# Moving due times in a hand-planned cross-attention and feed-forward kernel: when x1 is written, when the last batch is stored, and where each gathered head is loaded and split

## The chip, the cores and the metric

The kernel runs on one core of one Trainium2 chip. The metric is the device time of one execution in microseconds (us); lower is better. Engines: PE is TensorE, DVE VectorE, ACT ScalarE, POOL GpSimd, SP SyncE (here it only issues DMAs).

## The reference

Eight batches, each with x and ctx of 512 channels by 2048 columns, all float32. Per batch:

```
xn  = layernorm(x, over the 2048 columns)
t   = Wt @ ctx ;  p = Wp @ xn ;  g = Wg @ ctx            (xattn with q = xn, k = v = ctx)
att = sum over each group of 64 channels of p * g        (one number per group)
y   = Wz (per group) @ (att * t)
x1  = x + (y - mean)/sqrt(var) * gn_w + gn_b + ctx       (mean, var per group)
u   = layernorm(x1)[:, perm]          -> 16 heads of 128 columns
out = x1 + (gelu(u_h @ up_h) @ down_h)[:, unperm]        (up_h 128x512, down_h 512x128)
```

## The kernel before, in words

Every matrix product is made in float32 accuracy with three passes: both operands are split into a rounded high part (`_hi`, a copy on ACT) and the rest (`_lo`, a subtraction on DVE), and PE multiplies low by high, high by low and high by high. All products have 512 columns.

A batch i has two stages. In the attention stage PE builds S = x ctx^T over 16 slices of columns (`s_mm`), then y in four quarters (`y_mm`), then p·g through S (`v_mm`). Meanwhile Z holds y; after the group statistics (`g_mean`, `g_var_a`, `g_root` on POOL, `g_var_b`) DVE writes x1 into Z in eight pieces of 128x1024 (`x1_piece`, L1134), ACT squares them (`square_x1`, L959), and `sum_sq`, `root_x1`, `shift_x1`, `xln2` (L966) normalise. `turn` (L1159) transposes Z, four tiles for each of four quarters, and `store_x` writes the transposed batch to DRAM in four DMAs a quarter; from there single heads are gathered by the permutation. The stores of batches 0 to 6 are issued by POOL (L1246), those of batch 7 by SP (L1317).

The feed-forward stage follows each attention stage on PE. It works through groups g; a group is one head of one earlier batch: 16 groups in batches 2 to 6, 8 in batch 1, none in batch 0, and 40 in batch 7, which also has to finish its own heads. Weights of a head are used for two groups (two batches) while two batches are at hand, and for one group in most of batch 7. One group is, by engine:

- POOL: `gather` (indirect DMA of 256 KB from DRAM into a slot of FB, L1240), `resid` (a multiplication and an addition of 128x512, L1252 and L1255), `scatter` (indirect DMA to the output, L1260). A slot of FB is gathered anew six groups later, once its scatter has landed.
- ACT: `g_hi` (cast into GG, L973), and for each of two halves p `gelu` (two activations of 128x1024, L980 and L981).
- DVE: `g_lo` (L1164), two `h_lo` (L1169), `add_r` (L1175).
- PE: for each half six matmuls `up_mm` (L888) and six `dn_mm` (L903).
- SP: `load_w` (L1338) loads half the weights of a head (512 KB) as soon as the head two before has used that half; `load_x` (L1305) and `load_s` load the next batch's x, and its columns for S.

The order is not found at run time. The function `plan()` gives every task a due time in units (a unit is the time of 12 matmuls), sorts all tasks by it, and each engine's program is that list filtered to its own tasks, in order. Semaphores alone decide when a task starts; the due time only decides what it stands behind on its engine. Engines work strictly in order, so a task that waits holds all behind it. `base[i]` is the start of batch i, f0 = base[i] + 36 that of its feed-forward stage (464 for batch 7). Group g has its `up_mm` halves due at f0+2g-1 and f0+2g, its `dn_mm` halves at f0+2g+1.5 and f0+2g+2.5; `gelu` is due 0.6 and `h_lo` 1.2 units behind `up_mm`, `g_lo` at f0+2g-2.1.

`X1_UNIT[1 if i == 1 else 2 if last else 0]` says in the groups of which numbers the eight `x1_piece` stand: (2,3,5,6,8,10,11,13) for batches 2 to 6, (2,2,3,4,4,5,6,6) for batch 1 and (2..9) for batch 7. The piece is due at f0+3.25+2·number, which is right behind the second `h_lo` of group number+1.

Of the kernel before, what the change touches and what calls it, by code (L numbers as in the profile page):

```python
# [26 lines left out]
TURN = [(15.9, 19.0, 22.3, 25.5)] + [(10.2, 15.0, 19.6, 24.2)] * 6  # L27
# [2 lines left out]
S_EARLY = ([(-1 + 0.2 * dt, 0.5 + 0.2 * dt) for dt in range(4)],  # L30
           [(2.0, 2.5), (2.25, 2.75), (3.0, 3.25), (3.5, 3.75)])
S_LOAD = (-13, -10, -7, -2.8, -1, 3.2, 4.8, 6.8)
X1_UNIT = ((2, 3, 5, 6, 8, 10, 11, 13), (2, 2, 3, 4, 4, 5, 6, 6), (2, 3, 4, 5, 6, 7, 8, 9))
S_FIRST = ((-5.9, -4.9, -3.9, -2.9), (-9.9, -7.9, -5.9, -3.9))
S_LATE = {4: 2.55, 5: 2.8, 6: 3.3, 7: 4.4}

# [1 line left out]
def units(i):  # L38

    if i == 0:  # L40
        return []
    if i == 1:
        return [(h, [0]) for h in range(8, 16)]
    half = [8 * (i % 2) + h for h in range(8)]
    if i == 2:
        half = half[6:] + half[:6]
    ws = [(h, [i - 2, i - 1]) for h in half]
    if i == B - 1:
        rest = [8 * ((i + 1) % 2) + h for h in range(8)]
        ws += [(h, [i - 1]) for h in rest[:6]] + [(h, [i - 1, i]) for h in rest[6:]]  # L50
        ws += [(h, [i]) for h in range(ND) if h not in rest[6:]]
    return ws
# [20 lines left out]
def plan():  # L73
# [10 lines left out]
    def put(t, stage, *a):  # L84
        tasks.append((t, len(tasks), stage, a))
# [462 lines left out]
    for k in range(8):  # L548
        t = 15 + 2.6 * k
# [4 lines left out]
    for h in range(4):  # L554
        t = 38 + 4 * h
# [5 lines left out]
    base = [0, 36, 88] + [88 + 68 * k for k in range(1, B - 2)]  # L561
    f = 0
# [3 lines left out]
    for i in range(B):  # L566
        s0 = base[i]
        y0, v0, f0 = s0 + 16, s0 + 32, s0 + 36
        first = i == 0
        for k, h in enumerate((4, 5, 6, 7) if i == 2 else ()):  # L570
            put(y0 + (2.5, 5.2)[k // 2], load_raw, h)
            put(y0 + 5.6 + 1.8 * k, w_hi, h)
            put(y0 + 5.7 + 1.8 * k, w_lo, h)
            put(y0 + 5.8 + 1.8 * k, keep_w, h)
        for j in range(8):
            put(s0 + (S_LOAD[j] if i > 1 else 0.3 if (i, j) == (1, 2) else 2 * j - (5 if i or j else 10)), load_s, i, j)
        for dt in range(ND):
            t = s0 + (dt - 2.6 if i < 2 else S_FIRST[i > 2][dt] if dt < 4 else S_LATE.get(dt, dt - 2.6))
            put(t, s_hi, i, dt)
            put(t + 0.2, s_lo, i, dt)  # L580
            for c1 in range(NT):
                put(s0 + (dt + 0.25 * c1 if i < 2 or dt > 3 else S_EARLY[c1 // 2][dt][c1 % 2]), s_mm, i, dt, c1)
        for q in range(NQ):
            for ct in range(NT):
                t = s0 + 2.2 + 3.3 * ct + 0.8 * q if i == 2 else s0 + (4 * q + ct) * 0.85 + 0.9
                t = 10.4 + 1.4 * ct + 0.22 * q if first else s0 + 9.3 + 1.6 * ct + 0.4 * q if i == 1 else t
                put(t, bn_x, i, ct, q)
        if first:
            for ct in range(NT):
                put(5.4 + 1.7 * ct, load_x, i, ct)  # L590
        put(y0 + 2, aggr_x, i)
        put(y0 + 2.1, root_x, i)
        late = 1.0 if i == 1 else 0
        for q, t in enumerate((s0 + 9, s0 + 11, s0 + 13, y0 + 1.5 + late)):
            put(t, load_c, i, q)
        put(y0 + (9 if i == 2 else 2.5 + late), load_wg, i)
        for q, t in enumerate((y0 - 3, y0 + 0.4, y0 + 4.3, y0 + 8.3)):
            put(t, y_hi, i, q)
            put(t + 0.2, y_lo, i, q)
        for q, t in enumerate((y0 - 1, y0 + 1.2, y0 + 2.6, y0 + 4.6)):  # L600
            for ct in range(NT):
                put(t + 0.25 * ct + late, add_c, i, q, ct)
        put(y0 + 5.8 + late, sum_c, i)
        put(y0 + 5.9 + late, store_sum, i)
        put(y0 + 7.6 + late, spread_sum, i)
        for c1 in range(NT):
            put(y0 + 11.3 + 0.6 * c1, s_fix, i, c1)
            put(y0 + 11.5 + 0.6 * c1, s_evh, i, c1)
            put(y0 + 12.2 + 0.6 * c1, s_evl, i, c1)
        for q in range(NQ):  # L610
            for ot in range(NT):
                put(y0 + 4 * q + ot, y_mm, i, q, ot)
            for pr in range(2):
                t = y0 + 4 * q + 2 * pr + 2
                put(t, y_ev, i, q, pr)
                for e in range(2):
                    put(t + 0.6 + 0.5 * e, bn_y, i, q, 2 * pr + e)
        if i:
            put(y0 + 1, load_wph, i)
            put(y0 + 12.1, load_wpl, i)  # L620
        for ot in range(NT):
            put(v0 + ot + (0.5 if i and ot == NT - 1 else 0), v_mm, i, ot)
            put(v0 + ot + (1.4 if i and ot == NT - 1 else 0.95), v_att, i, ot)
        put(v0 + 3.4, aggr_y, i)
        put(f0 + 1.2, g_mean_mm, i)
        put(f0 + 1.25, g_mean, i)
        put(f0 + 2.3, g_var_mm, i)
        put(f0 + 2.35, g_var_a, i)
        put(f0 + 2.4, g_root, i)
        put(f0 + (3.9 if first else 5.25), g_var_b, i)  # L630


        last = i == B - 1
        for k in range(8):
            ct, hf = k // 2, k % 2
            t = f0 + 5 + 0.8 * k if first else f0 + 3.25 + 2 * X1_UNIT[1 if i == 1 else 2 if last else 0][k] + 0.01 * k
            put(t, x1_piece, i, ct, hf)
            put(t + (0.9 if first else 1.2) if first or last else base[i + 1] + 0.9 + 0.55 * k, square_x1, i, ct, hf)
            if hf and not last:
                put(base[2] - 1.5 + 3.3 * ct if i == 1 else t + 0.1, load_x, i + 1, ct)  # L640
        put(f0 + (4.1 if first else 5.26), mean_x1, i)
        e = f0 + 12 if first else f0 + 22.8 if last else base[i + 1] + 5.4
        put(e, sum_sq, i)
        put(e + 0.1, root_x1, i)
        put(e + 0.9, shift_x1, i)
        put(e + 1.2, store_sd, i)
        put(f0 + 30 if last else f0 + 29.5 if i == 0 else e + 5, spread_sd, i)
        for ct in range(NT):
            put(e + 1.1 + (0.6 if first else 1.8 if last else 0.9) * ct, xln2, i, ct)
        for q in range(NQ):  # L650
            t = base[i + 1] + TURN[i][q] if not last else e + 7.6 + 1.4 * q
            for ct in range(NT):
                put(t + 0.25 * ct, turn, i, q, ct)
            put(t + 1, store_x, i, q)


        ws = units(i)
        gs = [(b, h, x) for x, (h, bs) in enumerate(ws) for b in bs]
        end = len(gs)
        for g, (b, h, x) in enumerate(gs):  # L660
            lead = f0 + 2 * g
            put(max(lead - 6.5, v0 - 3 if g == 0 else v0 - 1), gather, f, b, h)
            put(lead - (2.45 if g else 3.0), g_hi, f, b)
            put(lead - (2.1 if g else 2.8), g_lo, f, b)
            put(lead - 2.05, resid, f, b)
            for p in range(2):
                kk = 2 * g + p
                left = 2 * end - kk
                tu = f0 + (kk - 1 if kk else -1)
                td = f0 + kk + 1.5  # L670
                if left < 3:
                    td = f0 + 2 * end + (-0.5 * left if last else (1.5, 0)[left - 1])
                put(tu, up_mm, f, p, UPS[(kk - 2 * end) % 3], w + x)
                put(tu + 0.6, gelu, f, p, kk, i)
                put(tu + 1.2, h_lo, f, p)
                put(td, dn_mm, f, p, w + x)
                w_used[w + x] = (tu + 0.55, td + 0.55)
            put(td + 0.45, add_r, f)
            put(td + 0.6, scatter, f, b, h)
            f += 1  # L680
        for x, (h, bs) in enumerate(ws):
            for j in range(2):
                if x < 2 and i == 2:
                    kept.append((w + x, j, h))
                    continue
                t = w_used[w + x - 2][j] if w + x > 1 else 0
                t = max(t, y0 + 7 + 2 * x) if x < 2 else t
                put(t, load_w, w + x, h, j)
        w += len(ws)
# [25 lines left out]
def build_in(nc, ctx, x, cx, xT, cT, Wt, WpT, Wg, WzT, gnw, gnb, up, down, perm, outs):  # L715
# [3 lines left out]
    def f32(ap):  # L719
        return ap.bitcast(F32)  # L720

    order, at, free, slot, total = plan()
    S = {name: ctx.enter_context(nc.semaphore("s_" + name)) for name in total}

# [680 lines left out]
```

## Time and profile before

| what | value |
|---|---|
| median of 3 runs | 1612.38 us (1607.69 to 1612.63) |
| the profiled execution | 1607.69 us, span of its instructions 1605.9 us |
| PE | 1518.3 us busy, 95% of the span, 6592 matmuls |
| DVE, ACT, POOL | 80%, 61%, 54% |
| DMA | 374.77 MB, mean 233 GB/s |

A busy share of 95% says that PE sets the time nearly everywhere; the rest is found by looking at where PE stands still, and who released it then.

### The profile page before, as it was taken

Reading aid. Unit: us, or ns where it says so; the run is one execution under the profiler, and the core shown is the slowest. Engines: PE = TensorE matmul, PEld = TensorE weight load, DVE = VectorE, ACT = ScalarE, POOL = GpSimd, SP = SyncE. Lnnn points to the kernel's source line nnn. Section 1 sums busy time; section 2 is a strip of 40 time slices with the busy share of each in tenths; the row PEclk is TensorE's granted clock in tenths of the full one; section 3 lists DMA queues with packets and bytes.
Section 4 is the critical chain, followed back from the end, with each engine's and each line's share of the span. In section 5 each row is a group of like instructions: output and inputs, shape, how many; then the busy total and the mean of one; then the engine's idle time right before and its main releaser. Section 6 shows DMA issues by size and latency. Waiting matters only on the chain.

```text
span 1605.9 us, 19290 instructions
## 1 busy us (share of the span) xinstructions
PE 1518.3 (95%) x6592; PEld 1234.1 (77%) x6592; DVE 1279.0 (80%) x1736; ACT 974.7 (61%) x1061; POOL 874.1 (54%) x765
## 2 busy tenths in 40 slices
PE   8998899999989999999999999899998999986997
PEld 6776677877878887788877888688886888765885
DVE  5878979696996879879797888968789697866664
ACT  4334538734776367763677537774487735985785
POOL 1284437157871268613784238832388125976784
PEclk9999999999999999999999999999999999998999
DMA  8788968686776747677386755848568584569685
GB/s 320 288 291 317 331 203 307 247 286 214 239 277 191 251 127 256 248 222 232 118 283 216 249 189 174 283 172 257 163 201 297 156 260 155 190 163 286 207 291 179
DMA packets 126288, 374.77 MB, mean 233 GB/s; under 512 B 24560, under 2 KB 32752, under 8 KB 118000
## 3 DMA queue, kind: packets, MB, share of 16 engines
q1 hardware_dynamic: 91888, 251.88, 47.3%
q0 software_dynamic: 34304, 121.66, 22.4%
q8 instruction: 54, 0.88, 0.2%
q14 instruction: 42, 0.34, 0.1%
HBM read 287.45 MB, written 86.03 MB: 233 GB/s over the span
## 4 chain that ended last, share of the span: by engine, by line
PE 45%; POOL 17%; DVE 17%; DMA 10%; issue 7%; ACT 3%; SPq 0%; POOLq 0%; DVEq 0%; ACTq 0%
PE PP L835 14%; PE PP L849 13%; PE PP L903 7%; PE PP L888 6%; POOL FB L1255 5%; PE PP L862 5%; POOL FB L1252 4%; POOL out L1260 4%; DMA FB<-xg_scratch,perm_sb 3%; DVE R L1017 3%; POOL FB L1240 2%; DVE X L1029 2%; DMA WW<-w_scratch 2%; DVE R L1169 2%; DVE Z L1134 2%
## 5 line engine op out<-in xcount | busy, mean ns | idle before, releaser
L888 PE MATMUL PP<-GG,WW 128*128 128x512 f32 x1536 | 394.2, 393 | 38.8 <-DVE GG L1164 23.4
L835 PE MATMUL PP<-R 128*128 128x512 f32 x1536 | 360.7, 394 | 18.0 <-DVE R L1017 16.2
L888 PEld LDWEIGHTS PP<-GG,WW 128*128 128x128 f32 x1536 | 286.8, 189 | 111.5 <-issue 50.4
L849 PE MATMUL PP<-R,WC 128*128 128x512 f32 x1536 | 352.8, 391 | 7.6 <-ACT Z L934 4.1
L835 PEld LDWEIGHTS PP<-R 128*128 128x128 f32 x1536 | 290.9, 190 | 83.1 <-issue 18.5
L849 PEld LDWEIGHTS PP<-R,WC 128*128 128x128 f32 x1536 | 288.9, 188 | 70.4 <-ACT Z L934 6.8
L903 PE MATMUL PP<-R,WW 128*128 128x512 f32 x1050 | 271.1, 394 | 12.4 <-DMA WW<-w_scratch 6.0
L981 ACT ACTIVATE PP<-PP 128x1024 f32<-128x1024 f32 x256 | 261.6, 1022 | 0.0
L1169 DVE TENSOR_TENSOR R<-PP,R 128x1024 fp32r<-128x1024 f32 x175 | 213.1, 1218 | 60.4 <-ACT PP L981 60.3
L980 ACT ACTIVATE R<-PP 128x1024 fp32r<-128x1024 f32 x175 | 179.7, 1027 | 125.5 <-PE PP L888 125.3
L903 PEld LDWEIGHTS PP<-R,WW 128*128 128x128 f32 x1050 | 195.6, 189 | 58.4 <-issue 17.3
L1017 DVE TENSOR_TENSOR R<-RAW,R 128x1024 fp32r<-128x1024 f32 x128 | 171.5, 1344 | 82.9 <-ACT R L922 82.6
L1260 POOL DMA_INDIRECT out<-FB,perm_sb x128 | 154.5, 1207 | 106.2 <-DVE FB L1175 91.2
L1255 POOL TENSOR_TENSOR FB<-FB,SMM 128x512 f32<-128x512 f32 x128 | 202.9, 1585 | 10.1
L1246 POOL DMA_DIRECT2D xg_scratch<-FB x104 | 68.5, 670 | 256.2 <-DVE FB L1159 256.2
L1252 POOL TENSOR_TENSOR FB<-FB,SMM 128x512 f32<-128x512 f32 x128 | 166.9, 1304 | 63.5 <-DVE GG L1164 50.6
L922 ACT CAST R<-RAW 128x1024 fp32r<-128x1024 f32 x128 | 130.4, 1041 | 97.2 <-PE PP L835 47.6
L1240 POOL DMA_INDIRECT FB<-xg_scratch,perm_sb x128 | 130.5, 1019 | 95.1 <-DMA xg_scratch<-FB 35.8
L934 ACT COPY Z<-PP 128x1024 f32<-128x1024 f32 x64 | 64.8, 1013 | 147.2 <-PE PP L849 139.3
L1175 DVE TENSOR_TENSOR FB<-PP,FB 128x512 f32<-128x512 f32 x128 | 87.6, 684 | 75.5 <-PE PP L903 75.0
L1164 DVE TENSOR_TENSOR GG<-FB,GG 128x512 fp32r<-128x512 f32 x128 | 122.9, 960 | 11.8 <-ACT GG L973 11.5
L903 PE MATMUL PP<-HX,WW 128*128 128x512 f32 x486 | 125.1, 393 | 0.4 <-DMA WW<-w_scratch 0.4
(91 smaller groups left out, 1639.4 us busy)
## 6 DMA issues: line engine op xcount, KB each, us to landing
WW<-w_scratch SPq DMA_DIRECT2D x152, 512.0 KB, 5.6
X<-in_x SPq DMA_DIRECT2D x32, 1024.0 KB, 5.5
RAW<-in_cx SPq DMA_DIRECT2D x32, 1024.0 KB, 9.2
RAW<-in_xT SPq DMA_DIRECT2D x63, 512.0 KB, 6.3
RAW<-in_cT SPq DMA_DIRECT2D x63, 512.0 KB, 8.6
xg_scratch<-FB POOLq DMA_DIRECT2D x104, 256.0 KB, 6.2
w_scratch<-WW POOLq DMA_DIRECT2D x16, 1024.0 KB, 5.7
RAW<-in_Wg SPq DMA_DIRECT2D x8, 1024.0 KB, 8.3
```

Of the source, the lines that this page charges most:

```text
L835: t = eng.matmul(s_bank(c1), l[:, part(c1)], r, start=(dt == 0 and j == 0), stop=(dt == ND - 1 and j == 2))
L849: t = eng.matmul(PP[2 + ot // 2][:, ot % 2, :], WC[:, l, ct, part(ot)], u[:, r + ct, :], start=(ct == 0 and j == 0), stop=(ct == NT - 1 an ...
L888: t = eng.matmul(PP[slot["up", f, p]][:, e, :], wt[:, l, part(2 * p + e)], g[:, r, :], start=(j == 0), stop=(j == 2))
L903: t = eng.matmul(PP[1][:, f % 2, :], wt[:, l, part(mt)], h_tile(f, p, r)[:, e, :], start=(mt == 0 and j == 0), stop=(mt == NM - 1 and j == 2))
L980: eng.activation(h_tile(f, p, 0), pp[:], ACT.Gelu).then_inc(S["hhi"], 1)
L981: eng.activation(pp[:], pp[:], ACT.Gelu).then_inc(S["gelu"], 1)
L1017: eng.tensor_tensor(s_tile(i, dt, 1), s_raw(i, dt), f32(s_tile(i, dt, 0)), ALU.subtract).then_inc(S["slo"], 1)
L1169: eng.tensor_tensor(h_tile(f, p, 1), PP[slot["up", f, p]][:], f32(h_tile(f, p, 0)), ALU.subtract).then_inc(S["hlo"], 1)
L1240: eng.indirect_dma_start(out=FB[:, f % NFB, :], out_offset=None, in_=xg_d[b][:, :], in_offset=perm_of(h)).then_inc(S[f"fb{f % NFB}"], 16)
L1252: eng.tensor_tensor(FB[:, f % NFB, :], FB[:, f % NFB, :], SM[b % 2][:, 0, :], ALU.mult).then_inc(S["rmul"], 1)
L1255: eng.tensor_tensor(FB[:, f % NFB, :], FB[:, f % NFB, :], SM[b % 2][:, 1, :], ALU.add).then_inc(S["radd"], 1)
L1260: eng.indirect_dma_start(out=outs[b][:, :], out_offset=perm_of(h), in_=FB[:, f % NFB, :], in_offset=None).then_inc(S[f"sc{f % NFB}"], 16)
```

## The change

Only due times change; no instruction is added, removed or altered. With f0 the start of the feed-forward stage:

- `x1_piece` is due at f0+7.25+step·k for its eight pieces k, with step 2 in batches 2 to 6, 1.2 in batch 1 and 1.33 in batch 7. The table X1_UNIT goes. (Batches 2 to 6 had 7.25, 9.26, 13.27, 15.28, 19.29, 23.3, 25.31, 29.32; they get 7.25, 9.25, ..., 21.25. Batch 7 had 7.25, 9.26, ..., 21.32; it gets 7.25, 8.58, ..., 16.56.)
- In batches 2 to 6 `load_x` of the next batch, due 0.1 behind every second piece, moves with it: from 9.36, 15.38, 23.4, 29.42 to 9.35, 13.35, 17.35, 21.35.
- In batch 7 `square_x1` stays 1.2 behind its piece; `sum_sq` goes from f0+22.8 to f0+18.4, and with it the rest of the second layer norm and `store_sd`; the quarters of `turn` go from f0+30.4+1.4q to f0+26+1.5q and `store_x` from f0+31.4+1.4q to f0+27+1.5q. `spread_sd` stays at f0+30.
- In every group `gather` goes from 6.5 to 6 ahead of the group's f0+2g, `g_hi` from 2.45 to 2.3 (group 0 of a batch stays), `resid` from 2.05 to 1.5.

```diff
-X1_UNIT = ((2, 3, 5, 6, 8, 10, 11, 13), (2, 2, 3, 4, 4, 5, 6, 6), (2, 3, 4, 5, 6, 7, 8, 9))
...
-            t = f0 + 5 + 0.8 * k if first else f0 + 3.25 + 2 * X1_UNIT[1 if i == 1 else 2 if last else 0][k] + 0.01 * k
+            t = f0 + 5 + 0.8 * k if first else f0 + 7.25 + (1.2 if i == 1 else 1.33 if last else 2) * k
             put(t, x1_piece, i, ct, hf)
             put(t + (0.9 if first else 1.2) if first or last else base[i + 1] + 0.9 + 0.55 * k, square_x1, i, ct, hf)
             if hf and not last:
                 put(base[2] - 1.5 + 3.3 * ct if i == 1 else t + 0.1, load_x, i + 1, ct)
...
-        e = f0 + 12 if first else f0 + 22.8 if last else base[i + 1] + 5.4
+        e = f0 + 12 if first else f0 + 18.4 if last else base[i + 1] + 5.4
...
-            t = base[i + 1] + TURN[i][q] if not last else e + 7.6 + 1.4 * q
+            t = base[i + 1] + TURN[i][q] if not last else e + 7.6 + 1.5 * q
...
-            put(max(lead - 6.5, v0 - 3 if g == 0 else v0 - 1), gather, f, b, h)
-            put(lead - (2.45 if g else 3.0), g_hi, f, b)
+            put(max(lead - 6, v0 - 3 if g == 0 else v0 - 1), gather, f, b, h)
+            put(lead - (2.3 if g else 3.0), g_hi, f, b)
             put(lead - (2.1 if g else 2.8), g_lo, f, b)
-            put(lead - 2.05, resid, f, b)
+            put(lead - 1.5, resid, f, b)
```

## Rows read from the trace of the kernel before

**Rows 1.** The page: busy time, share of the span, instructions of an engine.

```profile
PE 1518.3 (95%) x6592; PEld 1234.1 (77%) x6592; DVE 1279.0 (80%) x1736; ACT 974.7 (61%) x1061; POOL 874.1 (54%) x765
```

**Rows 2.** Waits of PE: engine, line, releaser, us in total, times, longest.

```profile
PE PP L888 <- DVE GG L1164: 23.4, 21, 2.5
...
PE PP L903 <- DMA WW<-w_scratch: 6.5, 4, 3.8
```

**Rows 3.** Windows, feed-forward of batch 4: PE, PEld, DVE, ACT, POOL busy, clock, DMA.

```profile
981.73:1058.00 76.27, 70.17 (x305) 56.60 (x304) 72.82 (x64) 58.84 (x68) 64.96 (x47) 1.00 0.73 252
```

**Rows 4.** Windows, feed-forward of batch 7, same columns.

```profile
1360.23:1414.37 54.14, 53.03 (x229) 42.25 (x228) 46.54 (x51) 48.40 (x61) 48.89 (x38) 1.00 0.54 177
1414.37:1450.36 35.99, 29.43 (x121) 21.98 (x122) 23.93 (x29) 32.28 (x34) 26.09 (x24) 1.00 0.70 168
1450.36:1486.29 35.93, 24.97 (x86) 18.09 (x84) 21.39 (x28) 15.26 (x17) 22.27 (x20) 0.81 0.94 297
1486.29:1596.41 110.12, 109.45 (x481) 89.69 (x479) 70.94 (x78) 85.35 (x96) 82.82 (x72) 1.00 0.73 244
```

**Rows 5.** Timeline of PE, batch 4: start, us, what, idle before and releaser.

```profile
983.09 1.52 PE L888 MATMUL PP<-GG,WW 128*128 128x512 f32 x6
984.45 1.52 PE L903 MATMUL PP<-R,WW 128*128 128x512 f32 x6
...
1036.67 1.61 PE L888 MATMUL PP<-GG,WW 128*128 128x512 f32 x6 [2.44 <-DVE GG L1164]
...
1043.83 1.63 PE L888 MATMUL PP<-GG,WW 128*128 128x512 f32 x6 [1.43 <-issue]
```

**Rows 6.** Timeline of DVE, batch 4.

```profile
1031.81 3.05 DVE L1134 SCALAR_TENSOR_TENSOR Z<-Z,sm,X 128x1024 f32<-128x1024 f32 x1
1034.77 1.75 DVE L1164 TENSOR_TENSOR GG<-FB,GG 128x512 fp32r<-128x512 f32 x1
```

**Rows 7.** Timeline of ACT, batch 4.

```profile
982.85 1.02 ACT L981 ACTIVATE PP<-PP 128x1024 f32<-128x1024 f32 x1
983.79 0.61 ACT L973 CAST GG<-FB 128x512 fp32r<-128x512 f32 x1
984.64 1.03 ACT L980 ACTIVATE HX<-PP 128x1024 fp32r<-128x1024 f32 x1 [0.24 <-PE PP L888]
```

**Rows 8.** Timeline of DVE, batch 7.

```profile
1432.90 1.48 DVE L1164 TENSOR_TENSOR GG<-FB,GG 128x512 fp32r<-128x512 f32 x1 [1.29 <-ACT GG L973]
...
1505.62 0.69 DVE L1175 TENSOR_TENSOR FB<-PP,FB 128x512 f32<-128x512 f32 x1 [0.88 <-PE PP L903]
1506.24 1.22 DVE L1169 TENSOR_TENSOR HX<-PP,HX 128x1024 fp32r<-128x1024 f32 x1
1507.38 0.68 DVE L1164 TENSOR_TENSOR GG<-FB,GG 128x512 fp32r<-128x512 f32 x1
```

**Rows 9.** Timeline of POOL, batch 7.

```profile
1508.93 1.31 POOL L1252 TENSOR_TENSOR FB<-FB,SMM 128x512 f32<-128x512 f32 x1
```

**Rows 10.** Timeline of SP, batch 7: the stores (L1317) among the weight loads.

```profile
1452.90 4.04 SPq L1317 DMA_DIRECT2D xg_scratch<-RAW  x4
1457.10 1.90 SPq L1338 DMA_DIRECT2D WW<-w_scratch  x1
1459.04 6.11 SPq L1317 DMA_DIRECT2D xg_scratch<-RAW  x4
```

**Rows 11.** Timeline of PE, batch 7.

```profile
1464.61 2.90 PE L903 MATMUL PP<-R,WW 128*128 128x512 f32 x6 [3.81 <-DMA WW<-w_scratch]
...
1505.42 1.52 PE L888 MATMUL PP<-GG,WW 128*128 128x512 f32 x6
```

**Rows 12.** All weight loads: from issue to landing, us.

```profile
DMA to landing us min/median/max: 3.6/5.6/12.4
```

**Rows 13.** Groups of instructions: line, form, count, busy us, mean ns of one.

```profile
L1134 DVE SCALAR_TENSOR_TENSOR Z<-Z,sm,X 128x1024 f32<-128x1024 f32 x64 | 115.3, 1807 | 0.0
...
L1159 DVE STREAM_TRANSPOSE RAW<-Z 128x512 f32<-128x512 f32 x16 | 10.5, 683 | 0.0
```

## The prediction

> **What bounds the kernel now.** The page comes first, to see which engine sets the time: PE is busy 95% of the span and DVE 80% [rows 1]. Only time in which PE stands still can be won, about 87 us, of which 9.5 lie behind the last matmul. The waits of PE come next, since they name who released it: on `g_lo` 23.4 us in 21 waits, `dn_mm` alone on head weights 6.5 us in 4 [rows 2]. Then windows over the feed-forward stages, because the change works there alone. In batch 4, 76.27 us hold 70.17 of PE: 6.1 us lost. DVE worked 72.82 of them and stood only 3.45, so here DVE paces PE [rows 3]; batches 2, 3, 5 and 6 have the same order and I take them alike. Last the timelines, for what stands behind what.
>
> The measure for batch 7 is the half group of 12 matmuls: six start at 983.09 and the next six at 984.45, so twelve take 2.72 us and a group 5.44 [rows 5]. The first window of [rows 4] holds 19 half groups (51.7 us) in 54.14: 2.5 lost. The second holds 10 (27.2) in 35.99: 8.8 lost. The third holds 7 (19.0) in 35.93: 16.9 lost, 11.0 of it idle and the rest at a granted clock of 0.81; six matmuls that start after 3.81 us of idleness take 2.90 us instead of 1.52 [rows 5, 11]. The fourth loses nearly nothing. The third window is where SP issues the stores of batch 7. Each quarter holds SP for 4.04 to 6.11 us, and weight loads leave only between them [rows 10].
>
> **The change part by part.** No work is added, so every term is a change of lost PE time.
>
> *x1 in batches 2 to 6.* Now the pieces stand behind groups 3, 4, 6, 7, 9, 11, 12 and 14, and the last three share their groups with `s_lo` (L1017), the preparation of the next batch. There the piece took 3.05 us, the `g_lo` behind it 1.75, and PE lost 2.44 and 1.43 us in the two waits that came of it [rows 5, 6]. Afterwards they stand behind groups 3 to 10 and never meet `s_lo`. A group with a piece costs DVE, summed from undisturbed rows, 0.68 (`g_lo`) + 2 × 1.22 (`h_lo`) + 0.69 (`add_r`) + 1.81 (the mean piece) = 5.6 us, about 5.2 as neighbours overlap by some 0.08; with the 1.75 of a disturbed `g_lo` it is 6.3 [rows 6, 8, 13]. Against 5.44 a group, eight in a row lose between nothing and 8 × 0.86 = 6.9 us, with no light group between for DVE to catch up, as groups 5, 8, 10 and 13 are now. I take 5.1 in place of 6.1, nearer to the upper end since pieces were disturbed more often than not: -1.0 a batch, **-5** in five. Lower bound: DVE's work is the same, so at most its idle 3.45 us a batch comes back, -17. Upper: 6.9 and up to 2 us in the `s_lo` groups, +2.8 a batch, +14.
>
> *load_x.* Its DMAs move earlier on SP's queue (`load_x` of quarters 2 and 3 in front of weights and `load_s`). Each waits for a piece due 0.1 before it, and behind it stand weights that are needed over 10 us later (each serves two groups). I cost it at nothing; without that cover it would cost what DVE is late, about 1 us a batch.
>
> *gather and resid.* On POOL the sequence scatter, gather, resid is kept. Only `g_root` goes ahead of the `resid` of group 2, which can hold that `resid` and all POOL work behind it by about 1.3 us once a batch (one tensor instruction [rows 9]); the gather behind it is due 4 groups ahead. Nothing, at most +1 a batch.
>
> *g_hi.* This swaps two entries on ACT in all but the first group of every stage: `g_hi` of group g was due 0.05 ahead of the first `gelu` of group g-1, now 0.1 behind. So a new path closes: the first `up_mm` of g-1 starts at 983.09, its gelu at 984.64; each activation takes 0.94 until the next starts, so `g_hi` starts at 986.52 in place of 983.79, ends at 987.13, and an undisturbed `g_lo` ends at 987.81. PE follows 0.15 us behind a `g_lo` (1034.77 + 1.75 to 1036.67), so at 987.96, and it is due at 983.09 + 5.44 = 988.53: 0.57 us to spare [rows 5 to 8]. But `g_lo` took 1.48 and 1.75 us where POOL was working on FB, and then it is 0.23 or 0.50 us late [rows 6, 8]. Does it meet POOL? In the steady end of batch 7 `g_lo` starts 1.96 us behind its group's `up_mm` and POOL's multiplication 3.51; `g_lo` goes to 4.04, into the multiplication's 1.31 us [rows 8, 9, 11]. Once it is late, though, so are `add_r`, the scatter and the next multiplication, and the next `g_lo` comes first. I take every second of the 20 groups after the stores: 10 × 0.23 = **+2.3** (0 to +10 at 0.50 each). In batches 2 to 6 DVE is late with `g_lo` anyway, and the bounds above hold it.
>
> *Batch 7, x1.* Eight pieces in 10.6 units (28.9 us) in place of 16. DVE: 5.3 groups × 3.5 + 8 × 1.81 = 33.0 us, 4.1 too many; less the 0.57 to spare, 3.5 lost in place of 2.5: **+1** (0 to +4). The squares crowd ACT likewise, beside it.
>
> *Batch 7, second layer norm.* The same instructions 4.4 units earlier among groups of the same kind: 8.8 lost as now, **0** (-2 to +2).
>
> *Batch 7, stores.* They go to 27, 28.5, 30 and 31.5, when a head's weights still serve two groups. Quarters 0 and 1 then stand ahead only of a load needed 4.45 units (12 us) after it is due. Quarters 2 and 3 still stand ahead of loads with 2.45 units, 6.7 us, of which landing takes 5.6 [rows 12]. If quarter 2 leaves SP 4.04 us after 29.75 to 30.5, its load lands 0.8 to 3 us late; quarter 3 the same once: 3 us together, and 1 for the clock. The 16 transposes are 10.9 us of DVE [rows 13] in 16.3 us that also hold three groups' 10.5: about 4.5 us too many, which the weights hide today. 8.5 lost in place of 16.9: **-8.4** (-15 to 0).
>
> *Batch 1.* The same eight pieces in the same eight groups: 0, within 1.
>
> Sum: -5 + 2.3 + 1 + 0 - 8.4 = -10.1 us. The profiled execution took 1607.69 us and would take 1597.6; it is the fastest of the three, and the median lies 4.7 above it, so the median goes from 1612.38 to **1602.3**.
>
> **The rivals.**
>
> *The ring of g_hi (slower).* `up_mm`, gelu, `g_hi`, `g_lo`, `up_mm` paces PE wherever `g_lo` meets POOL. Speaking for it: only 0.57 us to spare, and POOL works on FB for half of each group. Against: lateness moves POOL away. Eight groups in each of the five batches, 8 in batch 1 and 30 in batch 7 would be 78 × 0.23 = 18 us in place of my 2.3: +5.6, 1618; with part of them at 0.50, 1625. It decides from 12.4/0.23 = 54 groups on.
>
> *The stores collide anyway (no change).* DVE finishes the transposes so late that quarters 2 and 3 push the same weights: -1 in place of -8.4, the sum -2.7, 1609.7. For it: DVE's 4.5 us of excess. Against: two of four quarters have room.
>
> *DVE's idle time comes back whole (more).* -17 in place of -5, the sum -22: 1590. Against: nearly all groups of batches 2 to 6 are disturbed today.
>
> *A piece waits out a whole POOL instruction (much slower).* The piece at 1031.81 took 3.05 us; were all so, with `g_lo` at 1.75, a group would be 3.05 + 1.75 + 2.44 + 0.69 = 7.9 us, 2.5 over, 20 us in eight groups in place of 6.1: +68 over five batches in place of -5, 1675. Against: the mean piece is 1.81 [rows 6, 13]. The Trainium skill's page SBUF — State Buffer, section Who interferes with whom, states that a DVE instruction with two SBUF inputs and a GpSimd instruction that reads SBUF exclude each other, and the one that comes second blocks fully; by that rule an unlucky order would give this rival, and the trace agrees for single pieces only.
>
> **How the numbers follow.** Forecast 0.38, idle time back 0.08, no change 0.20, the ring 0.29, pieces blocked 0.05. Faster is 0.46, same 0.20, slower 0.34, with 0.3% (4.8 us) as what a measurement of this kernel can tell from none. The forecast's own range is 1594 to 1609. The range 1588 to 1625 reaches over the no-change case and nearly all of the ring, and leaves out the blocked pieces and the ends.
>
> **What would show it.** In the third window of batch 7 PE idles under 6 us and waits on weights under 3; the stores stand near 1430 to 1445 on SP. Groups 11 to 15 of batches 2 to 6 show no wait over 1 us, groups 6 to 10 several small ones on `g_lo`. The ring would show as six-matmul groups of L888 each 5.67 us apart with `g_lo` right behind `g_hi`, and as PE waits on `g_lo` in the end of batch 7, where there are none now. The prediction is wrong above all if those are many, or if DVE's instructions are disturbed more or less often in the new order, which no row fixes.

## The result and the profile after

The changed kernel takes 1622.59 us (median of 5 runs, 1620.82 to 1626.57), the kernel before 1612.38 beside it (1607.52 to 1614.9): a ratio of 1.0081, 95% interval 1.0062 to 1.0100. It is slower, and I had forecast faster. The profiled execution took 1625.33 us. Below line 33 every line of the changed kernel has a number lower by one: `g_lo` is L1163, `x1_piece` L1133, `g_hi` L972, `up_mm` L887, `g_root` L1229 and L1231, the two halves of `resid` L1251 and L1254, `scatter` L1259.

The page, the row that answers to [rows 1]: PE works 13.5 us more and POOL 12.9, with the same instructions.

```profile
PE 1531.8 (94%) x6592; PEld 1232.5 (76%) x6592; DVE 1289.8 (79%) x1736; ACT 975.0 (60%) x1061; POOL 887.0 (55%) x765
```

Where in the kernel was it lost? The two tiny matmuls of `g_mean_mm` stand once in each batch, so their start is a milestone. Here are those of batches 2 and 7, by source line (minimum, median and maximum in ns, first and last start), before:

```profile
L872 PE MATMUL PP<-am,avg x2: 170/213/256, 389.8 to 389.9; 128*128 128x8 f32 x2
...
L872 PE MATMUL PP<-am,avg x2: 170/213/256, 1352.9 to 1353.0; 128*128 128x8 f32 x2
```

and after:

```profile
L871 PE MATMUL PP<-am,avg x2: 170/213/256, 396.1 to 396.2; 128*128 128x8 f32 x2
...
L871 PE MATMUL PP<-am,avg x2: 173/214/256, 1370.9 to 1371.0; 128*128 128x8 f32 x2
```

From batch 2 to batch 7 is 963.1 us before and 974.8 after; from there to the end of the span 253.0 and 252.6. So batches 2 to 6 lose 11.7 us between these two executions and batch 7, where I had expected the gain, nets nothing. (The eight milestones before stand at 122.8, 238.5, 389.8, 582.8, 775.2, 967.6, 1160.6 and 1352.9 us. So the stretch behind 967.6, from which [rows 3] and [rows 5 to 7] are taken, is the feed-forward of batch 5 and not of batch 4; batches 2 to 6 have the same order, and no reading hangs on the name.) Batch 2 starts 6.3 us later, but this start varies by 6 us between profiled executions of kernels that are alike up to there (389.8, 393.3, 393.7, 395.8), and before had the earliest; I read nothing from it.

The waits of PE after, beside [rows 2]:

```profile
PE PP L887 <- issue: 16.1, 31, 1.7
PE PP L887 <- DVE GG L1163: 15.1, 19, 3.0
PE PP L887 <- DMA WW<-w_scratch: 11.1, 3, 8.4
```

The waits on `g_lo` fell from 23.4 to 15.1 us; those put down to "issue" rose from 10.3 to 16.1 and are mostly the same wait, as the timelines show. In batch 5 they stand in a regular pattern (PE timeline, changed kernel):

```profile
1013.75 1.62 PE L887 MATMUL PP<-GG,WW 128*128 128x512 f32 x6 [0.63 <-DVE GG L1163]
...
1019.98 1.63 PE L887 MATMUL PP<-GG,WW 128*128 128x512 f32 x6 [0.51 <-issue]
...
1026.31 1.63 PE L887 MATMUL PP<-GG,WW 128*128 128x512 f32 x6 [0.59 <-DVE GG L1163]
```

Six such waits follow each other from 1013.75 to 1045.11, so a group takes 31.36/5 = 6.27 us in place of 5.44. Of the 0.83 us lost only 0.5 to 0.6 are idle time; the rest is in matmuls that take longer behind a wait (1.62 us for six, 1.52 otherwise), which is why PE's busy time grew. What makes 6.28 is seen on DVE and POOL in the same stretch (DVE timeline, then POOL timeline):

```profile
1016.39 1.79 DVE L1133 SCALAR_TENSOR_TENSOR Z<-Z,sm,X 128x1024 f32<-128x1024 f32 x1
1018.10 1.78 DVE L1163 TENSOR_TENSOR GG<-FB,GG 128x512 fp32r<-128x512 f32 x1
1019.80 1.21 DVE L1168 TENSOR_TENSOR HX<-PP,HX 128x1024 fp32r<-128x1024 f32 x1
1020.94 0.67 DVE L1174 TENSOR_TENSOR FB<-PP,FB 128x512 f32<-128x512 f32 x1
1021.54 1.21 DVE L1168 TENSOR_TENSOR R<-PP,R 128x1024 fp32r<-128x1024 f32 x1
1022.67 1.79 DVE L1133 SCALAR_TENSOR_TENSOR Z<-Z,sm,X 128x1024 f32<-128x1024 f32 x1
```

```profile
1014.79 0.97 POOL L1239 DMA_INDIRECT FB<-xg_scratch,perm_sb  x1 [0.30 <-issue]
1015.78 1.30 POOL L1251 TENSOR_TENSOR FB<-FB,SMM 128x512 f32<-128x512 f32 x1
1017.16 2.17 POOL L1254 TENSOR_TENSOR FB<-FB,SMM 128x512 f32<-128x512 f32 x1
1019.49 1.28 POOL L1259 DMA_INDIRECT out<-FB,perm_sb  x1 [0.16 <-issue]
...
1022.07 1.30 POOL L1251 TENSOR_TENSOR FB<-FB,SMM 128x512 f32<-128x512 f32 x1
```

Neither engine stands: from one piece of x1 to the next DVE spends 6.28 us, from one multiplication to the next POOL 6.29. And the instructions are stretched in turn. The multiplication ends at 1017.08 and x1 at 1018.18, 1.10 later; the addition ends at 1019.33, 1.15 after x1; `g_lo` ends at 1019.88, 0.55 after the addition. Undisturbed they take 1.27, 1.29 and 0.68 us. So each does nearly all of its work only once the one before it is done, as if they took turns. By the Trainium skill, page SBUF — State Buffer, section Who interferes with whom, a DVE instruction with two SBUF inputs and a GpSimd instruction that reads SBUF exclude each other; the trace agrees. Before has this cycle too, in fewer groups (POOL timeline, kernel before):

```profile
1008.09 2.16 POOL L1255 TENSOR_TENSOR FB<-FB,SMM 128x512 f32<-128x512 f32 x1
```

The loop can be added up on POOL alone. From one multiplication to the next it is 1.30 us (the multiplication), 1.10 (until x1 ends), 1.15 (until the addition ends), 0.16 of gap, 1.28 (the scatter's issue), 0.31 of gap and 0.99 for the gather's issue: 6.29. With each instruction at its undisturbed length it would be about 5.1, less than PE's 5.44.

The window of batch 5 beside [rows 3], like that one 14.1 us behind `g_mean_mm`: POOL is busy 68.22 us in place of 64.96, DVE 72.31 in place of 72.82, and PE needs 70.87 in place of 70.17 for 300 matmuls in place of 305.

```profile
993.93:1070.20 76.27, 70.87 (x300) 54.96 (x299) 72.31 (x66) 58.89 (x67) 68.22 (x48) 1.00 0.77 270
```

And batch 7, beside [rows 4], windows after:

```profile
1378.30:1432.00 53.70, 48.38 (x205) 37.39 (x203) 47.54 (x50) 47.43 (x60) 48.52 (x39) 1.00 0.49 157
1432.00:1470.00 38.00, 35.01 (x138) 26.34 (x138) 29.44 (x39) 31.36 (x33) 27.63 (x24) 0.96 0.79 201
1470.00:1510.00 40.00, 29.94 (x122) 23.74 (x122) 19.73 (x24) 22.07 (x25) 23.93 (x22) 0.91 0.88 283
```

PE idles 5.3, 3.0 and 10.1 us in the three, against 1.1, 6.6 and 11.0 before (width less PE's busy time).

### The profile page after: what moved, and what is told of

Same layout as the page of the kernel before. It is cut to its first block, busy times and chain, and to the rows that moved or that the text cites. A ratio compares the mean times of both kernels' runs of the same rounds, so it can differ in the third digit from the quotient of the medians.

```text
span 1623.5 us, 19290 instructions
## 1 busy us (share of the span) xinstructions
PE 1531.8 (94%) x6592; PEld 1232.5 (76%) x6592; DVE 1289.8 (79%) x1736; ACT 975.0 (60%) x1061; POOL 887.0 (55%) x765
## 4 chain that ended last, share of the span: by engine, by line
PE 42%; DVE 17%; POOL 15%; DMA 11%; issue 8%; ACT 4%; SPq 2%; POOLq 0%; DVEq 0%; ACTq 0%
PE PP L848 12%; PE PP L834 10%; PE PP L902 8%; PE PP L887 8%; POOL FB L1254 5%; PE PP L861 5%; POOL FB L1251 4%; POOL FB L1239 3%; DVE X L1028 2%; DVE R L1016 2%; POOL out L1259 2%; DMA FB<-xg_scratch,perm_sb 2%; DMA X<-in_x 2%; DVE Z L1133 2%; DVE R L1022 2%
## 5 line engine op out<-in xcount | busy, mean ns | idle before, releaser
L887 PE MATMUL PP<-GG,WW 128*128 128x512 f32 x1536 | 399.4, 396 | 43.0 <-issue 16.1
L887 PEld LDWEIGHTS PP<-GG,WW 128*128 128x128 f32 x1536 | 283.9, 189 | 128.3 <-issue 67.8
L1163 DVE TENSOR_TENSOR GG<-FB,GG 128x512 fp32r<-128x512 f32 x128 | 136.5, 1066 | 115.7 <-ACT GG L972 111.0
L1254 POOL TENSOR_TENSOR FB<-FB,SMM 128x512 f32<-128x512 f32 x128 | 209.9, 1640 | 10.1
L1251 POOL TENSOR_TENSOR FB<-FB,SMM 128x512 f32<-128x512 f32 x128 | 167.4, 1308 | 77.4 <-DVE GG L1163 49.5
L1259 POOL DMA_INDIRECT out<-FB,perm_sb x128 | 158.2, 1236 | 81.9 <-DVE FB L1174 64.2
L921 ACT CAST R<-RAW 128x1024 fp32r<-128x1024 f32 x128 | 130.8, 1043 | 99.1 <-DMA RAW<-in_cT 50.2
```

What stands on the lines that cost most here:

```text
L887: t = eng.matmul(PP[slot["up", f, p]][:, e, :], wt[:, l, part(2 * p + e)], g[:, r, :], start=(j == 0), stop=(j == 2))
L1251: eng.tensor_tensor(FB[:, f % NFB, :], FB[:, f % NFB, :], SM[b % 2][:, 0, :], ALU.mult).then_inc(S["rmul"], 1)
L1254: eng.tensor_tensor(FB[:, f % NFB, :], FB[:, f % NFB, :], SM[b % 2][:, 1, :], ALU.add).then_inc(S["radd"], 1)
L1259: eng.indirect_dma_start(out=outs[b][:, :], out_offset=perm_of(h), in_=FB[:, f % NFB, :], in_offset=None).then_inc(S[f"sc{f % NFB}"], 16)
```

## The experiments

All ratios are to the kernel before, run on the same chip in five rounds, with the 95% interval. "Batches 2 to 6" is the time between the two milestones above in the one profiled execution. It is coarser than the ratio: with the order there unchanged it came to 963.1, 967.2, 968.1 and 970.3, so what a part costs is read from the ratios.

**1. The parts, each put alone into the kernel before.** The spacing of x1 in batches 2 to 6 (and `load_x` with it):

```diff
-  ... else f0 + 3.25 + 2 * X1_UNIT[1 if i == 1 else 2 if last else 0][k] + 0.01 * k
+  ... else f0 + 7.25 + 2 * k if 1 < i < B - 1 else f0 + 3.25 + 2 * X1_UNIT[1 if i == 1 else 2][k] + 0.01 * k
```

> One part of the change alone: x1 pieces of batches 2 to 6 behind groups 3 to 10, with load_x 0.1 behind them; all else as before. Theory A (consecutive pieces lock DVE and POOL into a common cycle of 6.28 us a group, as in groups 5 to 10 of batch 4 of the changed kernel): slower by 8 to 13 us in five batches, the cycle of 6.28 us visible. Theory B (the loss comes from g_hi standing behind gelu, the pieces are harmless): within 3 us of before, PE waits in groups 5 to 10 under 2 us in all.

The three head times (gather 6, g_hi 2.3, resid 1.5):

> One part alone: gather at 6, g_hi at 2.3, resid at 1.5 ahead of each group. Theory A: within 4 us of before, since a g_lo that comes later makes POOL's resid wait for it and the two no longer meet; no waits on g_lo in the steady end of batch 7. Theory B: slower by 8 to 18 us, waits of PE on g_lo of 0.2 to 0.5 us in most groups.

Batch 7 (step 1.33, 18.4, 1.5):

> One part alone: batch 7 with its x1 pieces 1.33 apart and the second layer norm, transposes and stores 4.4 units earlier. The changed kernel took as long as before from the group statistics of batch 7 to the end (252.5 against 252.9 us of span), so alone this part should be within 3 us of before. If the head times cost batch 7 something in the changed kernel, this part alone is faster by 3 to 9 us, and weight waits of PE sum to under 6 us.

Batch 1 (step 1.2):

> One part alone: x1 pieces of batch 1 spaced 1.2 instead of in the table's groups. In the changed kernel the stretch from batch 1's to batch 2's group statistics is 157.1 us against 151.3. If that is the pieces' spacing: slower by 3 to 6 us. If it is the head times or the timing of DMAs: within 2 us of before, and the loss shows in the run with the head times alone.

Measured: x1 0.9968 (0.9951 to 0.9984), faster by 5 us; head times 1.0099 (1.0069 to 1.0129), 978.9 us in batches 2 to 6; batch 7 0.9994 (0.9977 to 1.0010), tail 250.9; batch 1 1.0005 (0.9987 to 1.0022). The theory that eight pieces in neighbouring groups cost the time fell: their spacing alone gains (more than the 3 us of the other theory), though the cycle is there, as the PE timeline of that kernel shows (five waits, 1008.43 to 1033.60, of which one):

```profile
1014.75 1.62 PE L888 MATMUL PP<-GG,WW 128*128 128x512 f32 x6 [0.64 <-DVE GG L1164]
```

The loss is in the head times.

**2. Which head time.** The gather alone at 6 would stand behind the residual; of the three together, what remains in the orders is 121 swaps on ACT (`g_hi` behind a gelu) and 7 on POOL (`g_root` ahead of the residual of group 2, once in each of batches 1 to 7). Each alone:

```diff
-            put(lead - (2.45 if g else 3.0), g_hi, f, b)
+            put(lead - (2.3 if g else 3.0), g_hi, f, b)
```

> The kernel before with one number changed: g_hi 2.3 instead of 2.45 units ahead of its group, which puts it behind the gelu of the group before on ACT, and changes no other engine's order. Theory B1 (DVE can't run g_lo early any more and so can't catch up between the x1 pieces): slower by 12 to 18 us, nearly all of what the head times together cost; DVE waits on ACT for g_lo 60 to 110 us in all. Theory B2 (it is g_root ahead of resid, which makes POOL late): within 4 us of before.

```diff
-            put(lead - 2.05, resid, f, b)
+            put(lead - 1.5, resid, f, b)
```

> The kernel before with resid 1.5 instead of 2.05 units ahead, whose only effect on any order is that g_root stands ahead of the resid of group 2 on POOL, 7 times. Theory B1: within 4 us of before. Theory B2: slower by 10 us or more.

Measured: g_hi 1.0046 (1.0026 to 1.0066), which lies between its two theories, and g_root 1.0071 (1.0051 to 1.0091), as theory B2 had it. Seven entries on the engine that is busy least cost 11 us. The POOL timeline at the start of the feed-forward of batch 5, in the kernel before (`g_mean_mm` at 967.6):

```profile
971.14 1.30 POOL L1252 TENSOR_TENSOR FB<-FB,SMM 128x512 f32<-128x512 f32 x1 [4.16 <-DVE GG L1164]
972.51 1.30 POOL L1255 TENSOR_TENSOR FB<-FB,SMM 128x512 f32<-128x512 f32 x1
973.79 0.22 POOL L1230 TENSOR_SCALAR ve<-sm 128x4 f32<-128x4 f32 x1
974.09 1.05 POOL L1232 TENSOR_TENSOR rs<-ve,half 128x4 f32<-128x4 f32 x1
975.35 1.10 POOL L1260 DMA_INDIRECT out<-FB,perm_sb  x1 [0.21 <-issue]
```

and in the changed kernel (`g_mean_mm` at 979.8):

```profile
985.18 0.23 POOL L1229 TENSOR_SCALAR ve<-sm 128x4 f32<-128x4 f32 x1 [3.51 <-DVE sm L1100]
985.49 1.05 POOL L1231 TENSOR_TENSOR rs<-ve,half 128x4 f32<-128x4 f32 x1
986.53 1.28 POOL L1251 TENSOR_TENSOR FB<-FB,SMM 128x512 f32<-128x512 f32 x1
987.88 1.29 POOL L1254 TENSOR_TENSOR FB<-FB,SMM 128x512 f32<-128x512 f32 x1
989.35 1.36 POOL L1259 DMA_INDIRECT out<-FB,perm_sb  x1 [0.17 <-issue]
```

`g_root` waits for DVE's `g_var_a` (L1100). Before, the residual ran mostly inside that wait; now POOL stands through it with the residual queued behind, and the batch's first scatter starts 9.55 us after `g_mean_mm` in place of 7.75: 1.8 us late, and 1.7 (9.4) in the kernel with this swap alone. This lateness is never made good. Mean over batches 2 to 6, the sixteenth scatter starts 97.0 us after `g_mean_mm` before and 99.1 with the swap alone. The late `g_hi` shows on DVE: its waits for `g_hi` before `g_lo` go from 11.5 us in 5 to this row (waits of DVE, kernel with g_hi alone):

```profile
DVE GG L1164 <- ACT GG L973: 114.2, 66, 5.8
```

With it alone the first scatter is 0.5 us late (8.25) and the sixteenth 1.3 (98.3).

**3. Is the shared reading the bound?** The changed kernel with the residual's addition on 4 of 512 columns, so its output lacks the addition on the other 508:

```diff
-                eng.tensor_tensor(FB[:, f % NFB, :], FB[:, f % NFB, :], SM[b % 2][:, 1, :],
+                eng.tensor_tensor(FB[:, f % NFB, 0:4], FB[:, f % NFB, 0:4], SM[b % 2][:, 1, 0:4],
```

> The changed kernel, whose resid leaves out 508 of the 512 columns of its addition on POOL (the multiplication stays), so the output lacks most of the shift. It takes 1.2 us of POOL work with SBUF inputs out of each of 128 groups. If the common cycle of 6.28 us (x1 and g_lo on DVE, the multiplication and the addition on POOL shutting each other out) is what costs batches 2 to 6 their time, the cycle falls to 5.44 or little above and the kernel gets faster than before by 15 us or more. If DVE is late for its own work and its wait for g_hi alone, it stays within 5 us of the changed kernel.

Measured: 0.9758 (0.9726 to 0.9790), 38 us under before, 3.2% under the changed kernel; batches 2 to 6 take 935.3 us. The POOL timeline of this run:

```profile
1007.73 0.20 POOL L1254 TENSOR_TENSOR FB<-FB,SMM 128x4 f32<-128x4 f32 x1
...
1013.16 1.06 POOL L1254 TENSOR_TENSOR FB<-FB,SMM 128x4 f32<-128x4 f32 x1
```

and DVE beside the second of the two additions:

```profile
1012.69 1.48 DVE L1016 TENSOR_TENSOR R<-RAW,R 128x1024 fp32r<-128x1024 f32 x1
```

The cut addition takes 0.20 us (the median of all 128), so this run takes 1.09 us of POOL's own work out of each group as well as the collisions, and it can't tell one from the other. Where the addition met `s_lo`, which reads two SBUF tiles, it took 1.06 us and ended 0.05 after it. Pieces of x1 and `g_lo` are back at 1.27 and 0.69 us. PE has no wait in this stretch. The same cut in the kernel before:

> The kernel before with the residual's addition on 4 of 512 columns, as the changed kernel was run earlier (ratio 0.976 to before); the output lacks the addition on the other 508 columns. Theory: the two swaps cost only because GpSimd is the bound in batches 2 to 6, so with 1.3 to 2.2 us of it gone from each group they cost nothing, and this kernel runs within 0.3% of the changed one so treated: ratio 0.973 to 0.979, 1573 to 1582 us. Rival: the swaps cost by themselves (the residual held behind g_root, g_lo without a head start): this one is faster than the changed one so treated by the 1% of the full kernels: ratio 0.965 to 0.969.

Measured: 0.9797 (0.9777 to 0.9817), batches 2 to 6 935.6 us. That is 0.4% above the changed kernel so treated and just outside the theory's 0.973 to 0.979, but far from the rival's 0.965 to 0.969: with the shorter addition the new order is no slower than the old, though `g_root` still holds POOL (waits of POOL, changed kernel with the cut addition):

```profile
POOL ve L1229 <- DVE sm L1100: 36.1, 8, 4.6
```

A wait of POOL costs nothing by itself; it costs where POOL has no slack in which to make it good. How much it has is read from what it waits for. Take batch 5, from 12 to 88 us after `g_mean_mm`. In the kernel before, POOL waits there only for its own earlier scatters to land (four waits, 3.5 us in all), and those move with it when it is late; in the changed kernel it has nothing but its issue gaps of up to 0.31 us. With the cut addition it waits for DVE's `add_r` in nearly every group (POOL timeline, kernel before with the cut):

```profile
984.59 1.02 POOL L1260 DMA_INDIRECT out<-FB,perm_sb  x1 [0.92 <-DVE FB L1175]
```

The other reader taken away: in the changed kernel a piece of x1 reads Z alone (the addition of X is left out, so x1 lacks its residual term).

```diff
-                eng.scalar_tensor_tensor(out=Z[:, ct, cs], in0=Z[:, ct, cs], scalar=sm[:, 5, ct:ct + 1],
-                                         in1=X[:, ct, cs], op0=ALU.mult, op1=ALU.add).then_inc(S["x1"], 1)
+                eng.tensor_scalar(Z[:, ct, cs], Z[:, ct, cs], sm[:, 5, ct:ct + 1], None, ALU.mult).then_inc(S["x1"], 1)
```

> The changed kernel with x1_piece as a tensor_scalar multiplication that reads Z alone (the addition of X is left out, so x1 lacks its residual term); every place in the orders stays. Theory: what stretches GpSimd's addition from 1.29 to 2.16 us and x1 from 1.27 to 1.8 in batches 2 to 6 is that both engines read two SBUF inputs through one shared path, one instruction at a time. With one input x1 leaves that path and is short, the addition and g_lo meet only each other, the cycle of 6.28 us breaks up, and TensorE's waits of 0.5 us a group go: ratio 0.975 to 0.985, additions in the x1 part of 1.3 us mostly. Rival: the stretching comes from any traffic of the two engines together: x1 still 1.1 us or more, the addition still 1.6 us or more, and the ratio over 0.995.

Measured: 0.9971 (0.9952 to 0.9990), 1.1% under the changed kernel: a gain, but less than half of what I expected, and in the range of the rival, whose other two signs (x1 1.1 us or more, the addition 1.6 or more) came too. DVE timeline, and POOL's:

```profile
995.08 0.74 DVE L1133 TENSOR_SCALAR Z<-Z,sm 128x1024 f32<-128x1024 f32 x1
...
1011.84 1.26 DVE L1133 TENSOR_SCALAR Z<-Z,sm 128x1024 f32<-128x1024 f32 x1
1013.33 1.47 DVE L1163 TENSOR_TENSOR GG<-FB,GG 128x512 fp32r<-128x512 f32 x1 [0.23 <-ACT GG L972]
```

```profile
1011.23 1.31 POOL L1251 TENSOR_TENSOR FB<-FB,SMM 128x512 f32<-128x512 f32 x1
1012.62 1.63 POOL L1254 TENSOR_TENSOR FB<-FB,SMM 128x512 f32<-128x512 f32 x1
```

In this form x1 takes 0.74 us undisturbed (23 of the 64 pieces take 0.73 to 0.75), so the edit did two things: it took away one input and made x1 0.53 us shorter. And the 1.26 us is a disturbed piece: it ends 0.56 us after POOL's multiplication, and the addition ends 1.15 us after it, as in the changed kernel. So x1 still takes turns with POOL, and no run shows what a second input alone does. But the run shows how the cycle is made: it shrinks from 6.28 to 5.75 us, by just the 0.53 us that x1 got shorter, and is still above 5.44. In it DVE waits 0.2 to 0.7 us a group for `g_hi`, and POOL waits for nothing: the loop that sets the pace is POOL's.

**4. Undoing in the changed kernel.** First, g_hi at 2.45 and resid at 2.05 put back, gather left at 6:

> The changed kernel with two of its head times put back: g_hi at 2.45 and the residual at 2.05 units ahead of the group (so the gather's 6 and the spacings of x1 and batch 7 stay). Theory: the whole loss sits in these two swaps, and what is left is worth what its parts measured alone (spacing of x1 in batches 2 to 6 -0.3%, batch 7 and batch 1 nothing): ratio 0.995 to 0.999, 1605 to 1611 us, and periods of batches 2 to 6 of 192 to 193 us. Rival: the parts don't add, and the late x1 pieces of batches 2 to 6 together with the faster batch 1 and 7 cost something that none shows alone: ratio 1.002 or more, periods of 194 and over.

Measured: 1.0067 (1.0049 to 1.0085). It looked as if the parts didn't add, but it was my error: with the residual at 2.05, a gather at 6 falls behind it (114 gathers do). It is another reordering: the gather, which could run while POOL waits for `g_lo`, now runs after that wait. It costs 1.0067/0.9981 = 0.86% against the clean undoing, which comes next. All three put back:

> The changed kernel with all three head times put back (gather 6.5, g_hi 2.45, residual 2.05). Putting back only the last two left the gather at 6, and the residual then stands ahead of the gather of two groups later in GpSimd's order (all groups but the first few of a batch), where kernel before and changed kernel both have the gather first: that run was another reordering of GpSimd, which cost 0.67%, and no clean undoing. Theory: with GpSimd's order as before the loss is gone: ratio 0.995 to 0.999, 1605 to 1611 us, periods of batches 2 to 6 of 192 to 193 us. Rival: the parts don't add, and the spacing of x1 with batches 1 and 7 costs something in the whole that none shows alone: ratio 1.002 or more.

Only `g_root` put back behind the residual (its due time 2.55 in place of 2.4):

```diff
-            put(f0 + 2.4, g_root, i)
+            put(f0 + 2.55, g_root, i)
```

> The changed kernel with g_root put at 2.55 units instead of 2.4, so that it stands behind the residual of the third group of a batch again, as before; nothing else in any engine's order changes (7 swaps). Theory: the swap of g_root is the larger part of the loss (alone it measured 0.71%, g_hi alone 0.46%): ratio to before 0.999 to 1.004, 1611 to 1618 us, and the scatter of the batch's first group about 1.6 us earlier after the g_mean matmul than in the changed kernel (9.4 to 9.6 us there). Rival: g_hi late alone is enough for the locked cycle of 6.28 us, and nothing comes back: ratio 1.006 to 1.009.

Measured: all back 0.9981 (0.9961 to 1.0000), g_root back 1.0017 (1.0003 to 1.0031). So the whole loss is in the head times, and in the whole kernel `g_root` is worth 1.0081/1.0017 = 0.64% and the late g_hi 1.0017/0.9981 = 0.36%, each to about 0.25% either way. The first scatter of batch 5 comes 7.75 us after `g_mean_mm` with all back (as before) and 8.3 us with g_root back, 1.3 us earlier than in the changed kernel, where I had expected 1.6.

**5. A faster version.** Batch 7 with its stores given more room than the change gives them:

```diff
-            put(t + 1, store_x, i, q)
+            put(f0 + (27, 28.5, 30.6, 33.1)[q] if last else t + 1, store_x, i, q)
```

> The batch 7 part alone, with the stores of quarters 2 and 3 moved from 30 and 31.5 to 30.6 and 33.1, each right behind a weight load instead of ahead of it. If SP, held by a store that waits for its transposes, is what makes the weights late, the weight waits of PE in batch 7 fall under 3 us and the kernel is 5 to 9 us faster than before. If the DMA engines themselves are too full to bring the weights in time, it stays within 3 us of before.

Measured: 0.9971 (0.9946 to 0.9995), 5 us at the edge of the 5 to 9 that I expected, tail 248.3 us, and the longest wait for weights 4.37 us, not under 3. With the spacing of x1 in batches 2 to 6 as well:

> The kernel before with even spacing of x1 in batches 2 to 6 alone, and batch 7 of the changed kernel with its first four stores at 27, 28.5, 30.6 and 33.1 units. If the two gains seen apart (ratios 0.997 and 0.997) add: ratio 0.993 to 0.996, 1601 to 1606 us, periods of batches 2 to 6 192 to 192.5 us and a tail (first g_mean matmul of batch 7 to the end) of 248 to 249 us. Rival: one of the two was drift between runs: ratio 0.997 or more.

Measured: 0.9965 (0.9948 to 0.9983), tail 247.3, batches 2 to 6 965.7. It beats both kernels, but it falls short of the 0.993 to 0.996 of two gains that add, and the interval doesn't set it above either part alone. And with g_hi earlier still, at 3.45:

> The kernel of the two gains together, and with g_hi of each group moved ahead: at 3.45 units, ahead of the second gelu of the group before last in ScalarE's order instead of behind it. Only ScalarE's order changes. Theory: g_hi late takes from VectorE the chance to run g_lo early and catch up; if it still waits for g_hi now and then with g_hi at 2.45 (5 us in the whole kernel), an earlier one gives back at most those: ratio to the two gains together 0.997 to 1.000. Rival: a g_hi ahead of the gelu makes gelu 0.5 us later, so h_lo and the second down projection wait: ratio 1.003 or more against the two together, with waits of TensorE for h_lo.

Measured: 0.9986 (0.9971 to 1.0002), between the two expectations. Its PE waits on `g_lo` are down to 2.2 us in 6 (13.5 us in 14 without the move); the first entry of the list is now

```profile
PE PP L903 <- DVE R L1169: 14.6, 19, 2.2
```

DVE runs `g_lo` early and is late with `h_lo` instead. The same work on a full engine: the wait changes its name.

## Why the prediction was wrong

*g_root: the step that failed most, because POOL was taken to have room.* I wrote that it "can hold that `resid` and all POOL work behind it by about 1.3 us once a batch" and costed it at "Nothing, at most +1 a batch". It is worth 0.64 to 0.71%, 10 to 11 us, 1.5 us in each of the seven batches. Two errors: I priced the instruction and not its wait for `g_var_a`, so 1.3 us, where `resid` now starts 3.2 us later behind `g_mean_mm` and the scatter behind it 1.8; and I took POOL, busy 54% of the span, for an engine with room. [rows 3] had it at 64.96 of 76.27 us without its issue gaps, and the 0.15 to 0.30 us of these around each DMA fill much of the rest. The scatters show that the lateness stays through the whole stage (1.7 us at the first, 2.1 at the sixteenth, swap alone). The cut additions show that it is free once POOL has over 1 us of room in each group; that the collisions and not POOL's own work fill that room is worked out from the timelines (6.28 us against about 5.1 undisturbed) and not shown by a run of its own.

*g_hi.* I found the right path (`up_mm`, gelu, `g_hi`, `g_lo`) and looked for its price where nothing else disturbs, in the end of batch 7; there PE never waited on `g_lo`, so the +2.3 was nothing. For batches 2 to 6 I wrote "DVE is late with `g_lo` anyway, and the bounds above hold it". The price is there: measured 0.36 to 0.46%, 6 to 7 us. The likely way is that a DVE that is behind gains on light groups by running `g_lo` early, and a late `g_hi` takes that away (111.0 us of DVE waits in 68 after, 11.5 in 5 before); this is read from the waits and not tested apart.

*DVE paces PE in batches 2 to 6.* Half right. DVE was full because its instructions waited for POOL's, and the loop that set the pace was POOL's, with x1 and `g_lo` in it. What delays either engine there is paid.

*x1 in batches 2 to 6: -5.* Right, and for the reason given: 0.9968. The two late waits of a batch where a piece met `s_lo` (1.4 to 2.4 us each) are gone in that kernel, the small ones on `g_lo` take their place, and PE's waits before `up_mm` fall from 4.8 to 3.5 us a batch, where I had 6.1 to 5.1 for all of its loss. *Batch 1: 0* and *load_x: 0*: no run shows a cost; load_x was never moved alone.

*Batch 7.* By the prediction's own measure (a half group of 12 matmuls in 2.72 us) the three windows hold about 17, 11.5 and 10 half groups and lose 7.5, 6.7 and 12.8 us, where they lost 2.5, 8.8 and 16.9. So x1, +1, came to about +5, the second layer norm, 0, to -2, and the stores, -8.4, to -4: all three mis-sized (each figure is good to about a half group), by amounts that nearly cancel, and the part alone measured 0.9994, -1 us. That is the size of my rival of stores that collide anyway. SP's timeline shows the collision:

```profile
1455.18 9.24 SPq L1316 DMA_DIRECT2D xg_scratch<-RAW  x8
1464.58 2.01 SPq L1337 DMA_DIRECT2D WW<-w_scratch  x1
1466.94 1.21 SPq L1363 DMA_DIRECT2D SMM<-vq_scratch  x1
1468.20 3.86 SPq L1316 DMA_DIRECT2D xg_scratch<-RAW  x4
1472.22 2.05 SPq L1337 DMA_DIRECT2D WW<-w_scratch  x1
1474.31 7.49 SPq L1316 DMA_DIRECT2D xg_scratch<-RAW  x4
```

Quarters 0 and 1 hold SP for 9.24 us in one piece and push everything behind them. Quarter 3, due 4.5 units (12 us) after quarter 0, starts 19 us after it, and a weight load that leaves at 1472.22 holds PE for 8.44 us (PE timeline):

```profile
1480.51 2.90 PE L887 MATMUL PP<-GG,WW 128*128 128x512 f32 x6 [8.44 <-DMA WW<-w_scratch]
```

I had spaced the quarters by their due times and given 4.04 us to one of them, where four take 20.6. With the last two quarters 0.6 and 1.6 units later the longest wait fell from 10.65 us (batch 7 alone) to 4.37, and the tail from 250.9 to 248.3.

*The sum.* Measured apart: x1 -0.32%, head times +0.99%, batch 7 -0.06%, batch 1 +0.05%, together +0.66%, inside the interval of the whole. The time, 1622.59, lies in my range and near the rival of the ring, but that is luck for the most part: what the ring is made of, a late g_hi, carries about a third of the loss, and not in the way described; `g_root`, in none of my rivals, carries the rest.

Open: why the time of batches 2 to 6 differs between executions by up to 7 us (963.1 to 970.3 with their order unchanged), what the late g_hi would cost alone with the shorter addition, and what the collisions cost apart from POOL's own work. Neither of the last two was tried.

## What to carry to other kernels

An order change is priced by its wait and not by its instruction: list what each moved entry waits for, what is queued behind it, and how much work used to run inside that wait. Whether the engine can make it good is read in the window of that stage, as busy time plus its issue gaps, not from its share of the page. When DVE and GpSimd both read SBUF heavily in one loop, lay their instructions out as one chain: the stretched ones show as busy time on both, and here a piece of x1 that was 0.53 us shorter made the whole loop 0.53 us shorter. And look up the undisturbed length of an instruction that you altered before you read its time beside others.

## What the runs showed of the hardware

- x1, 1.27 us undisturbed, took 1.79 behind a POOL multiplication, POOL's addition 2.17 in place of 1.29, `g_lo` 1.78 in place of 0.68, each ending about its own length after the one before it. DVE's `h_lo`, which reads PSUM and one SBUF tile, took 1.18 to 1.23 us in all its 256 instructions in the changed kernel, beside POOL's work or not.
- A piece of x1 as `tensor_scalar` with one SBUF input took 0.74 us undisturbed and 1.26 beside POOL's multiplication, so it was held up too.
- An addition on 4 columns took POOL 0.20 us, one on 512 columns 1.29; behind a DVE instruction with two SBUF inputs the small one took 1.06.
- POOL's issue of an indirect DMA grew too: 1.02 us undisturbed, 1.28 where `g_lo` ran over its start (1019.49, above) and 1.82 at 1000.03 in the changed kernel, where a piece of x1 ran until 1000.96. Both end 0.89 us after the DVE instruction.
- After 8.44 us of idle time PE's next six matmuls took 2.90 us in place of 1.52, and the granted clock of that window was 0.91.
